# A fused linear-attention and expert layer: first and last batch reordered

## Chip, core and metric

One NeuronCore of a Trainium2 chip runs the whole program. The metric is the device time of one execution in microseconds (us), as the median of several executions. Engines are named as the profile names them: PE is TensorE, with PEld its weight loads; DVE is VectorE; ACT is ScalarE; POOL is GpSimd; SP is SyncE, which only issues DMAs here. All five run their own instruction streams and meet only at semaphores.

## What is computed

The input is x, 8 sequences x 2048 tokens x 256 channels, fp32. For each token:

```python
xn  = (x - mean(x)) / sqrt(var(x) + 1e-5)                 # over the 256 channels
q, k, v = split(xn @ wqkv);  q, k = relu(q), relu(k)      # 16 heads of 16
kv  = cumsum(k[..., :, None] * v[..., None, :], tokens)   # causal linear attention
y   = einsum('bhnd,bhnde->bhne', q, kv) / (einsum('bhnd,bhnd->bhn', q, cumsum(k)) + 1e-5)
s   = sigmoid(xn @ Wr)                                    # router, 8 experts, top 2, normalised -> cw
routed = sum over 4 MLP experts e of cw[e] * ((silu(xn @ Wg[e]) * (xn @ Wu[e])) @ Wd[e])
       + (cw[4] + cw[6]) * xn + cw[7] * relu(xn)
out = x + y @ wo + routed + causal_depthwise_conv4(xn)
```

## The kernel before

**Tiling.** The 16384 tokens go in 32 batches of 512 tokens (`BT`), four to a sequence; a batch is `T = 4` tiles of 128 tokens. Channels are `C = 2` halves of 128. `batch(s, j, left)` runs batch j of sequence s on each engine, and is written out by hand in program order for each engine (line 212, `rounds`). In each, the argument `k` of a helper says how far ahead of the batch it works: `heads(s, j, 1)` projects the next batch's queries, keys and values while the current one's output is being made.

**Precision.** Every fp32 product is made of three passes on fp32r data: each operand is split into a high part (ACT copies it, `high_weights`, `high_x`, `high_y`, `high_hid`) and a low part (the difference, `low_weights` on DVE; `low_x`, `low_y`, `low_hid` on POOL). `product` (line 296) issues the passes.

**A batch on PE** (lines 452 to 466): for each of the four tiles or experts t, `gate_up(t)` (12 matmuls of 512 columns), then `numerators(t)` (`state_sum`, 64 small matmuls with the masked scores, `state_sum`, 16 with the state). After tile 0 come the second half of the scores, after tile 1 the transposes of the next batch's xn (`turn_xn`). Then `heads` of the next batch, and four times `output(t)`: two transposes of the convolution `cT`, six matmuls with `wo`, twelve with `wd`. `state_sum(n)` waits until DVE has spread the running state into `state_bd` (`blocks(n)`).

**A batch on DVE** (lines 797 to 825): per tile `blocks`, `gate_up` (the product of silu and up), `blocks`, `attend` (line 792, numerator times inverse), and then in tile 0 `mask` of the second half of the scores (line 753), in tiles 1 to 3 `tap` (line 775, the convolution). Then, for later batches, `statistics` (line 689), `router`, `key_sums`, `products`, and between the final adds (line 825, `xb`) `inverses`, `mask`, `blocks`.

**A batch on ACT** (lines 559 to 577) does silu, the high parts, copies out of PSUM and the first tap; `heads` ends with the `same` terms (524), the relu terms (528, written over xn) and the denominators (531). **POOL** (lines 638 to 656) normalises the next batch, weighs the experts with `cwb` (626), makes low parts, and in `base` (614, 617) adds the terms into `x_t`.

**Ahead of the first batch.** SP issues, in this order, the first x block, tables, `wqkv` and router weights, three small tensors, gate and up weights, `wd`, `wo`, and x blocks 1 to 3. DVE runs `statistics` of batch 0, then `statistics` of batch 1 (line 836, which waits for x block 1), then all eight low parts of weights (839), then router, key sums, products, inverses, mask, blocks of batch 0. ACT makes the high parts of qkv weights, evicts the transposed xn (`fill_xT`), makes its high part from that, makes the other high weights, and goes on with `heads`. POOL normalises batch 0 after its own `rstd` (597), and makes `xl` (607). PE transposes xn (310), waits for the four qkv low parts (471), and runs `heads`.

**Behind the last batch.** PE's `output(0)` begins when all three taps are done (line 438); `x_t` of the batch is stored with one DMA of 512 KB (line 284) after the fourth final add.

Of the kernel before, what the change touches and what calls it, by code (L numbers as in the profile page):

```python
# [12 lines left out]
P = 128  # L13


def layer_kernel(nc, x, wqkv, wo, w_router, router_bias, w_gate, w_up, w_down, conv_w, conv_b,
# [28 lines left out]
    with ExitStack() as ctx:  # L45
# [31 lines left out]
        xn = sb("xn", [P, T, D])  # L77
# [91 lines left out]
        s_xn = sem("s_xn")  # L169
        s_xtr = sem("s_xtr")  # L170
# [68 lines left out]
        OWN_HEADS = 10 + 1 + 2 + 1  # L239
        OWN_SETUP = 2 * 2 + OWN_HEADS  # L240
        OWN_BODY = 2 + OWN_HEADS

# [3 lines left out]
        def _(sp):  # L246
            sp.dma_start(x_t[:, 0], x_v[0]).then_inc(x_in[0], 16)
            sp.dma_start(tables_s[:, :], tables).then_inc(tables_in, 16)
            sp.dma_start(st_r, w_router.rearrange("(c p) n -> p c n", p=P)).then_inc(qkv_in, 16)
            for c in range(C):  # L250
                sp.dma_start(st_qkv[:, c, :], wqkv[c * P:(c + 1) * P, :]).then_inc(qkv_in, 16)
            sp.dma_start(conv_ws[:, :, :], conv_w).then_inc(small_in, 16)
            sp.dma_start(conv_bs[:, :], conv_b).then_inc(small_in, 16)
            sp.dma_start(bias_s[:, :], router_bias).then_inc(small_in, 16)
# [5 lines left out]
            sp.dma_start(st_o, wo.rearrange("(c p) n -> p c n", p=P)).then_inc(out_in, 16)  # L260
            for j in range(1, BPS):
                sp.dma_start(x_t[:, j], x_v[j]).then_inc(x_in[j], 16)
# [16 lines left out]
            def batch(s, j, left):  # L279
# [3 lines left out]
                sp.wait_ge(s_out, at(s, j, T, 2 * T))  # L283
                sp.dma_start(out_v[b], x_t[:, j]).then_inc(stored, 16)
                sp.wait_ge(stored, at(s, j, 16, 16))
# [7 lines left out]
        def _(pe):  # L293
            mm = nc.tensor.matmul

            def product(dst, pairs, first=True, final=True):

                passes = [q for lh, ll, rh, rl in pairs for q in ((lh, rl), (lh, rh), (ll, rh))]
                for n, (lhs, rhs) in enumerate(passes):
                    ins = mm(dst, lhs, rhs, start=first and n == 0, stop=final and n == len(passes) - 1,  # L300
                             skip_group_check=not first)
                return ins

            def turn_xn(s, j, k, c):
                pe.wait_ge(s_xn, at(s, j, 1, k + 1))
                if k:

                    pe.wait_ge(s_sm, at(s, j, U * ROWS, U * ROWS))
                for t in range(T):
                    ins = nc.tensor.transpose(XB[c][:, t * P:(t + 1) * P], xn[:, t, c * P:(c + 1) * P], ident_s[:, :])  # L310
                ins.then_inc(s_xtr, 1)

            def heads(s, j, k):
# [15 lines left out]

                for g in range(C):  # L330
# [44 lines left out]
            def batch(s, j, left):  # L375
# [52 lines left out]
                def output(t):  # L428
# [8 lines left out]
                    if t == 0:  # L437
                        pe.wait_ge(s_conv, at(s, j, HALO, HALO))
                    for c in range(C):
                        mm(dst[:, c * P:(c + 1) * P], cT[:, c, ts], ident_s[:, :], is_transpose=True,  # L440
                           start=c == 0, stop=False, skip_group_check=True)
                    pe.wait_ge(s_yl, at(s, j, T, t + 1))
                    product(dst[:, 0:D], [(yh[:, c, ts], yl[:, c, ts], wo_h[:, c, :], wo_l[:, c, :])
                                          for c in range(C)], first=False, final=False)
                    for e in range(E):
                        if t == 0:
                            pe.wait_ge(s_hl, at(s, j, T, e + 1))
                        ins = product(dst[:, 0:D], [(hh[:, e, ts], hl[:, e, ts], wd_h[:, e, :], wd_l[:, e, :])],
                                      first=False, final=e == E - 1)
                    ins.then_inc(s_op, 1)  # L450
# [28 lines left out]
        def _(act):  # L479
# [25 lines left out]
            def heads(s, j, k):  # L505
# [13 lines left out]
                for g in range(C):  # L519
                    act.wait_ge(s_ktr, at(s, j, C, k * C + g + 1))  # L520
                    copy(ktok[:, :, g, :], KTB[g][:, :].rearrange("p (t n) -> p t n", t=T)).then_inc(s_ktok, 1)
                act.wait_ge(s_cw, at(s, j, 1, k + 1))
# [379 lines left out]
```

## Time and profile before

| | us |
|---|---|
| median of 3 runs (lowest, highest) | 1341.93 (1341.53, 1344.34) |
| the profiled execution's own time | 1342.8 |
| its span in the profile | 1341.0 |
| PE busy | 1310.1 (98%) |
| DVE busy | 1116.7 (83%) |
| POOL busy | 826.3 (62%) |
| ACT busy | 739.3 (55%) |

The span is from the first to the last recorded instruction or transfer; the own time has 1.8 us more around it. The chain that ended last is 97% PE. In the 40 slices PE shows 9 tenths in all but the first two (3, 8) and the last (7). A row of the timeline gives start, length, engine, line, operation, output<-input, shape, count, and in brackets the idle time of the engine before it and what ended it; the length of a merged row is from its first start to its last end.

### The profile page before, as it was taken

To read this page: it belongs to the slowest core of one execution; us is meant where nothing else is said; L and a number is where in the kernel's file an instruction comes from. 1 tells how busy PE (TensorE), PEld (TensorE's weight loads), DVE (VectorE), ACT (ScalarE), POOL (GpSimd) and SP (SyncE) were. 2 spreads that over 40 slices of the span, in tenths; PEclk is the share of its full clock that TensorE was granted. 3 is DMA by queue.
4 is the path that set the end of the run, shared out by engine and by line. 5 is a ranking of instruction groups with operands and counts; after the bars stand their busy time and mean duration, and the time that the engine had idled before them with its cause. 6 is when DMAs were issued, how large, how long until landed. Compare 5 with 4: busy or idle time off the path is not lost.

```text
span 1341.0 us, 54748 instructions
## 1 busy us (share of the span) xinstructions
PE 1310.1 (98%) x24384; PEld 1136.4 (85%) x24384; DVE 1116.7 (83%) x2566; ACT 739.3 (55%) x1545; POOL 826.3 (62%) x679
## 2 busy tenths in 40 slices
PE   3899999999999999999999999999999999999997
PEld 3788888888888888888888888888888888888886
DVE  4888898888888888988888988889888889888885
ACT  4555565455664565654556655555645556555561
POOL 2755666755766656657556666557576566575554
PEclk9999999999999999999999999999999999999999
DMA  4011111111111111011111111111112110111110
GB/s 148 34 66 65 51 48 34 66 65 66 44 55 34 66 66 64 35 38 61 66 65 50 50 35 65 66 65 37 63 34 66 65 64 35 34 65 50 50 49 18
DMA packets 46779, 73.73 MB, mean 55 GB/s; under 512 B 6480, under 2 KB 42192, under 8 KB 42448
## 3 DMA queue, kind: packets, MB, share of 16 engines
q1 hardware_dynamic: 46544, 70.24, 15.1%
q8 instruction: 191, 3.13, 1.0%
q14 instruction: 44, 0.36, 0.1%
HBM read 53.18 MB, written 17.04 MB: 52 GB/s over the span
## 4 chain that ended last, share of the span: by engine, by line
PE 97%; DVE 1%; SPq 1%; ACT 1%; DMA 1%; issue 0%; DVEq 0%
PE ring L300 51%; PE scores L300 17%; PE ring L408 7%; PE ring L424 6%; PE scores L357 5%; PE state_sum L371 4%; PE ring L440 2%; PE scores L310 2%; PE scores L339 2%; DMA x_t<-in_L_attn_x_dram 1%; SPq L257 0%; DVE cT L775 0%; DVE sm L753 0%; ACT qp L517 0%; ACT xn L528 0%
## 5 line engine op out<-in xcount | busy, mean ns | idle before, releaser
L626 POOL TENSOR_TENSOR hid<-hid,cwb 128x512 f32<-128x512 f32 x128 | 171.5, 1340 | 228.8 <-DVE hid L783 228.1
L775 DVE SCALAR_TENSOR_TENSOR cT<-xT,conv_ws,cT 128x512 f32<-128x512 f32 x192 | 292.9, 1564 | 0.0
L614 POOL TENSOR_TENSOR x_t<-x_t,same 128x1024 f32<-128x1024 f32 x32 | 77.0, 2406 | 258.6 <-ACT same L524 258.6
L760 DVE TENSOR_TENSOR state_bd<-state_sum,tables_s 128x256 f32<-128x256 f32 x248 | 103.7, 418 | 136.1 <-PE state_sum L371 136.1
L540 ACT ACTIVATE sg<-ring 128x512 f32<-128x512 f32 x128 | 76.6, 599 | 250.8 <-PE ring L300 250.8
L300 PE MATMUL ring<-xl,wgu_h 128*128 128x512 f32 x512 | 212.1, 414 | 0.0
L630 POOL TENSOR_TENSOR hl<-hid,hh 128x512 fp32r<-128x512 f32 x128 | 208.1, 1626 | 0.0
L300 PE MATMUL ring<-xh,wgu_l 128*128 128x512 f32 x512 | 202.7, 396 | 0.0
L300 PE MATMUL ring<-xh,wgu_h 128*128 128x512 f32 x512 | 202.0, 394 | 0.0
L480 ACT ACTIVATE yh<-yT 128x256 fp32r<-128x256 f32 x128 | 53.5, 418 | 247.3 <-DVE yT L792 247.3
L753 DVE TENSOR_TENSOR sm<-scores,causal_s 128x512 f32<-128x512 f32 x256 | 158.5, 679 | 22.3 <-PE scores L357 22.3
L300 PE MATMUL ring<-wd_h,hl 128*128 128x256 f32 x512 | 143.8, 281 | 0.0
L300 PE MATMUL ring<-wd_h,hh 128*128 128x256 f32 x512 | 143.6, 280 | 0.0
L300 PE MATMUL ring<-wd_l,hh 128*128 128x256 f32 x512 | 143.4, 280 | 0.0
L635 POOL TENSOR_TENSOR yl<-yT,yh 128x256 fp32r<-128x256 f32 x128 | 130.2, 1017 | 0.0
L408 PE MATMUL ring<-sm,vp 64*32 64x64 f32 x8192 | 118.8, 225 | 0.0
L300 PEld LDWEIGHTS ring<-xl,wgu_h 128*128 128x128 f32 x512 | 96.7, 189 | 24.5 <-issue 5.5
L300 PEld LDWEIGHTS ring<-xh,wgu_l 128*128 128x128 f32 x512 | 96.5, 188 | 22.4
L300 PEld LDWEIGHTS ring<-xh,wgu_h 128*128 128x128 f32 x512 | 97.1, 190 | 17.4
L371 PEld LDWEIGHTS state_sum<-vp,ktok 64*32 64x32 f32 x3968 | 54.1, 107 | 56.7 <-issue 51.5
L408 PEld LDWEIGHTS ring<-sm,vp 64*32 64x32 f32 x8192 | 98.1, 105 | 2.9 <-issue 2.9
L300 PE MATMUL scores<-xh,wqk_l 128*128 128x512 f32 x256 | 100.2, 392 | 0.0
(110 smaller groups left out, 3530.3 us busy)
## 6 DMA issues: line engine op xcount, KB each, us to landing
cwb<-cw_rows SPq DMA_DIRECT2D x32, 1024.0 KB, 4.6
x_t<-in_L_attn_x_dram SPq DMA_DIRECT2D x32, 512.0 KB, 4.3
out_dram<-x_t SPq DMA_DIRECT2D x32, 512.0 KB, 2.9
cw_rows<-cwt SPq DMA_DIRECT2D x128, 2.0 KB, 1.4
sm<-in_L_attn_wqkv_dram SPq DMA_DIRECT2D x2, 384.0 KB, 5.3
sm<-in_L_ffn_Wg_dram SPq DMA_DIRECT2D x2, 256.0 KB, 4.4
sm<-in_L_ffn_Wu_dram SPq DMA_DIRECT2D x2, 256.0 KB, 5.7
cwb<-in_L_ffn_Wd_dram SPq DMA_DIRECT2D x1, 512.0 KB, 4.4
```

What stands on the lines that cost most here:

```text
L300: ins = mm(dst, lhs, rhs, start=first and n == 0, stop=final and n == len(passes) - 1, skip_group_check=not first)
L371: ins = mm(ST[rows, g, :], ktok[toks, t, g, rows], vp[toks, t, g * PPG + m, 0:3:2, :], start=first and g == 0, stop=True, skip_group_check ...
L408: mm(NB2[t % 2][h][BLK * m:BLK * m + BLK, gs], window, sm[toks, t // 2, t % 2, 2 * pair + par, :], start=par == 0 and g == 0, stop=False, ...
L424: ins = mm(NB2[t % 2][h][rows, g * HALF:(g + 1) * HALF], state_bd[:, n % 4, cols], qT[:, g, n0:n0 + HALF], start=False, stop=True, skip_gr ...
L540: act.activation(sg[:, :], GB[t % 2], ACT.Silu).then_inc(s_sg, 1)
L614: pool.tensor_tensor(xb, xb, same[:, :, :], ALU.add).then_inc(s_base1, 1)
L626: pool.tensor_tensor(hid[:, e, :], hid[:, e, :], cwb[:, e, :], ALU.mult).then_inc(s_hid, 1)
L630: pool.tensor_tensor(hl[:, e, :], hid[:, e, :], hh[:, e, :].bitcast(F32), ALU.subtract).then_inc(s_hl, 1)
L635: pool.tensor_tensor(yl[:, :, t * P:(t + 1) * P], yT[:, t % 2, :, :], yh[:, :, t * P:(t + 1) * P].bitcast(F32), ALU.subtract).then_inc(s_y ...
L753: dve.tensor_tensor(heads, SB[f][:, :].rearrange("p (t a n) -> p t a n", a=2, n=HALF), causal2_s[:, :].unsqueeze(1).unsqueeze(1).to_broadc ...
L760: dve.tensor_tensor(state_bd[:, n % 4, :].rearrange("p (g m n) -> p g m n", g=C, m=PPG), ST.unsqueeze(2).to_broadcast([P, C, PPG, BLK]), s ...
L775: ins = dve.scalar_tensor_tensor(out=cT[:, c, :], in0=xT[:, j % 2, c, n:n + BT], scalar=conv_ws[:, c, n:n + 1], in1=cT[:, c, :], op0=ALU.m ...
```

## The change

- SP loads x block 0 and waits for it before it issues gate, up, `wd`, `wo`, the small tensors and x blocks 1 to 3. ACT issues tables, `wqkv` and router weights itself, at its start.
- `xn` has two halves, used by batches in turn. DVE normalises batch 0 tile by tile; PE transposes each tile as it comes. DVE and ACT evict the transposed xn from PSUM in parallel, `xT` by DVE and `xh` by ACT straight from PSUM, in opposite order of the halves. DVE makes `xl`.
- PE starts `heads` of batch 0 with two low parts of weights done and waits for the other two ahead of the keys.
- ACT runs one sigmoid on zeros at the start.
- `statistics` of batch 1 moves behind all low parts of weights; POOL normalises batch 1 ahead of `base` of batch 0 (in all later batches `normalise` stands at the end of a batch, behind `base`, where it stood at the beginning of the next).
- In batch 0, `inverses` moves from ahead of the first mask to a place between `blocks` and `attend` of tile 0; ACT's denominators follow silu(0), its relu terms follow the first tap.
- In the last batch, tap 3 goes ahead of `attend(3)`; `output(0)` adds the hidden products first, then the convolution, then the attention; the four tiles are stored one by one.

```diff
-        xn = sb("xn", [P, T, D])
+        xn = sb("xn", [P, 2, T, D])
...
             sp.dma_start(x_t[:, 0], x_v[0]).then_inc(x_in[0], 16)
-            sp.dma_start(tables_s[:, :], tables).then_inc(tables_in, 16)
-            sp.dma_start(st_r, w_router.rearrange("(c p) n -> p c n", p=P)).then_inc(qkv_in, 16)
-            for c in range(C):
-                sp.dma_start(st_qkv[:, c, :], wqkv[c * P:(c + 1) * P, :]).then_inc(qkv_in, 16)
-            sp.dma_start(conv_ws[:, :, :], conv_w).then_inc(small_in, 16)
...
+            sp.wait_ge(x_in[0], 16)
             for src, dst in ((w_gate, st_g), (w_up, st_u)):
...
+            sp.dma_start(conv_ws[:, :, :], conv_w).then_inc(small_in, 16)
...
+                    for t in range(T):
+                        sp.wait_ge(s_out, at(s, j, T, T + t + 1))
+                        sp.dma_start(out_v[b][:, t, :], x_t[:, j, t, :]).then_inc(stored, 16)
+                    sp.wait_ge(stored, at(s, j, 16, 16 * T))
...
+            def turn_first():
+
+                for t in range(T):
+                    pe.wait_ge(s_xn_tile, t + 1) if t < T - 1 else pe.wait_ge(s_xn, 1)
+                    for c in range(C):
+                        ins = nc.tensor.transpose(XB[c][:, t * P:(t + 1) * P], xn[:, 0, t, c * P:(c + 1) * P],
+                                                  ident_s[:, :])
+                        if t == T - 1:
+                            ins.then_inc(s_xtr, 1)
...
+                if not k:
+                    pe.wait_ge(w_split, EARLY)
                 for g in range(C):
                     project(KB[g][:, :], D + g * P).then_inc(s_kp, 1)
...
+                    late = last and t == 0
...
+                    if late:
+                        add_hidden()
+                        turn_conv()
+                        add_attention().then_inc(s_op, 1)
+                    else:
+                        turn_conv()
+                        add_attention()
+                        add_hidden().then_inc(s_op, 1)
...
-            for c in range(C):
-                turn_xn(0, 0, 0, c)
-            pe.wait_ge(w_split, EARLY)
+            turn_first()
+            pe.wait_ge(w_split, 2)
             heads(0, 0, 0)
...
                 silu(0)
+                if s == j == 0:
+                    denominators(0, 0, 0)
                 first_tap()
+                if s == j == 0:
+                    relu_terms(0, 0, 0)
...
+            act.dma_start(tables_s[:, :], tables).then_inc(tables_in, 16)
+            for c in range(C):
+                act.dma_start(st_qkv[:, c, :], wqkv[c * P:(c + 1) * P, :]).then_inc(qkv_in, 16)
+            act.dma_start(st_r, w_router.rearrange("(c p) n -> p c n", p=P)).then_inc(qkv_in, 16)
+            act.wait_ge(set_up, 3)
+
+            act.activation(sg[:, 0:1], zeros[:, 0:1], ACT.Sigmoid)
...
             high_weights(SPLITS[:EARLY])
-            act.wait_ge(set_up, 3)
-            fill_xT(0, 0, 0)
-            high_x(0, 0, 0)
+            for c in range(C):
+                act.wait_ge(s_xtr, c + 1)
+                if c:
+
+                    act.wait_ge(s_xT, 1)
+                copy(xh[:, 0, c, :], XB[c][:, :]).then_inc(s_xh, 1)
             high_weights(SPLITS[EARLY:])
...
-                if not last:
-                    normalise(s, j, 1)
                 weigh(0)
...
                 if not last:
                     base(s, j, 1)
+                if left > 1:
+                    normalise(s, j, 2)
...
-            normalise(0, 0, 0)
-            for c in range(C):
-                low_x(0, 0, 0, c)
-            pool.wait_ge(tables_in, 16)
+            inverse_deviation(0, 0, 0)
+            normalise(0, 0, 1)
             base(0, 0, 0)
...
+                    if s == j == t == 0:
+                        inverses(0, 0, 0)
+                    early = last and t == T - 1
+                    if early:
+                        tap(t)
                     attend(t)
                     if t == 0:
                         mask(s, j, 0, 1)
-                    else:
+                    elif not early:
                         tap(t)
...
             statistics(0, 0, 0)
-            statistics(0, 0, 1)
...
-            low_weights(0, N_SPLITS)
-            dve.wait_ge(small_in, 16 * 3)
+            dve.wait_ge(s_rstd, 1)
+            for t in range(T):
+                dve.tensor_scalar(xn[:, 0, t, :], x_t[:, 0, t, :], negm[:, t:t + 1], rstd[:, t:t + 1], ALU.add,
+                                  ALU.mult).then_inc(s_xn_tile if t < T - 1 else s_xn, 1)
+            low_weights(0, 2)
+            for c in (1, 0):
+                dve.wait_ge(s_xtr, C)
+                if c == 0:
+
+                    dve.wait_ge(s_xh, 1)
+                ins = dve.tensor_scalar(xT[:, 0, c, HALO:HALO + BT], XB[c][:, :], 1.0, None, ALU.mult)
+                ins.then_inc(s_xT, 1)
+            for c in range(C):
+                dve.wait_ge(s_xT, C)
+                dve.wait_ge(s_xh, c + 1)
+                dve.tensor_tensor(xl[:, 0, c, :], xT[:, 0, c, HALO:HALO + BT], xh[:, 0, c, :].bitcast(F32),
+                                  ALU.subtract).then_inc(s_xl, 1)
+            low_weights(2, N_SPLITS)
...
+            dve.wait_ge(small_in, 16 * 3)
+            statistics(0, 0, 1)
             router(0, 0, 0)
             key_sums(0, 0, 0)
             products(0, 0, 0)
-            inverses(0, 0, 0)
             mask(0, 0, 0, 0)
             blocks(0, 0, 0, 1)
```

## Rows read from the trace of the kernel before

**Rows 1.** Stretch of one batch: us, busy time of each engine, clock, DMA share, GB/s.

```profile
81.70:122.50 40.80, 40.80 (x770) 35.40 (x769) 35.16 (x80) 22.83 (x48) 25.55 (x22) 1.00 0.16 54
```

**Rows 2.** Waits of PE over the span: total us, times, longest us.

```profile
PE scores L310 <- POOL xn L600: 10.0, 1, 10.0
PE scores L300 <- DVE wqk_l L833: 9.3, 1, 9.3
PE ring L440 <- DVE cT L775: 3.1, 1, 3.1
PE scores L357 <- ACT ktok L480: 2.3, 1, 2.3
...
```

**Rows 3.** Timeline of the first 27 us, all engines.

```profile
4.30 1.41 DVE L689 BATCH_NORM_STATS2 stats<-x_t 128x6 f32<-128x256 f32 x4 [4.30 <-DMA x_t<-in_L_attn_x_dram]
...
7.68 2.16 POOL L600 TENSOR_SCALAR xn<-x_t,negm,rstd 128x256 f32<-128x256 f32 x4
...
8.97 0.63 ACT L480 ACTIVATE wvr_h<-sm 128x512 fp32r<-128x512 f32 x1 [6.97 <-DMA sm<-in_L_attn_wqkv_dram]
...
9.98 1.94 PE L310 MATMUL scores<-tables_s,xn 128*128 128x128 f32 x8 [9.98 <-POOL xn L600]
...
12.45 1.14 ACT L480 ACTIVATE xh<-xT 128x512 fp32r<-128x512 f32 x2
...
15.68 1.06 ACT L480 ACTIVATE wd_h<-cwb 128x1024 fp32r<-128x1024 f32 x1 [0.20 <-DMA sm<-in_L_attn_wo_dram]
...
17.19 1.41 DVE L689 BATCH_NORM_STATS2 stats<-x_t 128x6 f32<-128x256 f32 x4 [10.79 <-DMA x_t<-in_L_attn_x_dram]
...
23.39 1.22 DVE L833 TENSOR_TENSOR wd_l<-cwb,wd_h 128x1024 fp32r<-128x1024 f32 x1
...
26.79 0.19 DVE L700 TENSOR_TENSOR scoreb<-score,bias_s 128x32 f32<-128x32 f32 x1 [1.20 <-ACT score L509]
```

**Rows 4.** Timeline of DVE, 33 to 50 us.

```profile
34.92 1.28 DVE L738 TENSOR_REDUCE den<-qks_tok 128x32 f32<-128x512 f32 x2
38.24 0.55 DVE L744 RECIPROCAL rden<-dene 128x64 f32<-128x64 f32 x1 [2.04 <-ACT dene L531]
...
40.05 2.44 DVE L753 TENSOR_TENSOR sm<-scores,causal_s 128x512 f32<-128x512 f32 x4
...
45.73 2.48 DVE L753 TENSOR_TENSOR sm<-scores,causal_s 128x512 f32<-128x512 f32 x4 [0.68 <-PE scores L357]
49.00 0.42 DVE L760 TENSOR_TENSOR state_bd<-state_sum,tables_s 128x256 f32<-128x256 f32 x1 [0.79 <-PE state_sum L371]
```

**Rows 5.** Timeline of PE, 42 to 50 us.

```profile
42.98 0.25 PE L371 MATMUL state_sum<-vp,ktok 64*32 64x32 f32 x7 [2.17 <-DVE state_bd L760]
...
45.62 0.51 PE L300 MATMUL ring<-xl,wgu_h 128*128 128x512 f32 x1
...
49.48 0.33 PE L371 MATMUL state_sum<-vp,ktok 64*32 64x32 f32 x16
```

**Rows 6.** Timeline of DVE and POOL behind the last attention tile.

```profile
1323.36 2.61 DVE L775 SCALAR_TENSOR_TENSOR cT<-xT,conv_ws,cT 128x512 f32<-128x512 f32 x2
...
1323.70 1.71 POOL L630 TENSOR_TENSOR hl<-hid,hh 128x512 fp32r<-128x512 f32 x1
...
1326.51 1.28 POOL L630 TENSOR_TENSOR hl<-hid,hh 128x512 fp32r<-128x512 f32 x1
```

**Rows 7.** The chain that ended last, in order of time: PE in `output(0)`.

```profile
1326.77 3.24 PE ring L300 x18
```

**Rows 8.** DMA issues of the page: count, KB each, median us to landing.

```profile
out_dram<-x_t SPq DMA_DIRECT2D x32, 512.0 KB, 2.9
cw_rows<-cwt SPq DMA_DIRECT2D x128, 2.0 KB, 1.4
```

**Rows 9.** Timeline of DVE in a middle batch, tile 3.

```profile
711.33 0.42 DVE L760 TENSOR_TENSOR state_bd<-state_sum,tables_s 128x256 f32<-128x256 f32 x1 [0.33 <-PE state_sum L371]
...
712.92 3.40 DVE L775 SCALAR_TENSOR_TENSOR cT<-xT,conv_ws,cT 128x512 f32<-128x512 f32 x2
```

More of the change, by code:

```diff
@@ L300, in product @@
                     ins = mm(dst, lhs, rhs, start=first and n == 0, stop=final and n == len(passes) - 1,
-                             skip_group_check=not first)
+                             skip_group_check=not (first and final))
                 return ins
@@ L436, in output @@
                         pe.wait_ge(s_sig, at(s, j, T, T + 2 + t))
-                    if t == 0:
-                        pe.wait_ge(s_conv, at(s, j, HALO, HALO))
-                    for c in range(C):
[L440 to L444, printed above, removed]
@@ L445, in output, with turn_conv @@
-                    for e in range(E):
-                        if t == 0:
[L447 to L450, printed above, removed]
+                    late = last and t == 0
+                    def turn_conv():
+                        if t == 0:
+                            pe.wait_ge(s_conv, at(s, j, HALO, HALO))
+                        for c in range(C):
+                            mm(dst[:, c * P:(c + 1) * P], cT[:, c, ts], ident_s[:, :], is_transpose=True,
+                               start=c == 0 and not late, stop=False, skip_group_check=True)
@@ new lines, in add_hidden, with add_attention @@
+                    def add_hidden():
+                        for e in range(E):
+                            if t == 0:
+                                pe.wait_ge(s_hl, at(s, j, T, e + 1))
+                            ins = product(dst[:, 0:D], [(hh[:, e, ts], hl[:, e, ts], wd_h[:, e, :], wd_l[:, e, :])],
+                                          first=late and e == 0, final=e == E - 1 and not late)
+                        return ins
+                    def add_attention():
+                        pe.wait_ge(s_yl, at(s, j, T, t + 1))
+                        return product(dst[:, 0:D], [(yh[:, c, ts], yl[:, c, ts], wo_h[:, c, :], wo_l[:, c, :])
+                                                     for c in range(C)], first=False, final=late)
@@ L667, in _, with own @@
         def _(dve):
-            count = {"setup": 0, "body": 0, "in_body": False}
-            def own(ins, s, j, apart=False):
+            steps = itertools.count(1)
+            def own(ins, apart=False):
                 ins.then_inc(s_own, 1)
-                if not count["in_body"]:
-                    count["setup"] += 1
-                    dve.wait_ge(s_own, count["setup"])
-                else:
-                    count["body"] += 1
-                    dve.wait_ge(s_own, s * (BPS * OWN_BODY) + (j * OWN_BODY + count["body"] + OWN_SETUP))
+                dve.wait_ge(s_own, next(steps))
                 if apart:
@@ L725, in key_sums @@
                                                  before, ALU.add, ALU.add)
-                own(ins, s, j)
+                own(ins)
             def products(s, j, k):
@@ L743, in inverses @@
                 dve.wait_ge(s_dene, at(s, j, 1, k + 1))
-                own(dve.reciprocal(rden[:, :, :], dene[:, :, :]), s, j)
+                own(dve.reciprocal(rden[:, :, :], dene[:, :, :]))
                 for g in range(C):
@@ L825, in batch @@
                     dve.tensor_tensor(xb, OB[t][:, 0:D], xb, ALU.add).then_inc(s_out, 1)
-                if left > 1:
-                    assert count["body"] == OWN_BODY, count
             def low_weights(first, stop):
```

78 lines of the change are left out of this document (44 added, 34 removed).

## The prediction

> **What bounds the kernel now.** I read the busy times first, then the busy time of single batches, then PE's waits, then the timelines of the first 50 us and of the last 20. A middle batch takes 40.80 us and PE is busy for all of it, at a granted clock of 1.00 [rows 1]. PE's list of waits has five entries in the whole span, each met once: 10.0, 9.3, 3.1 and 2.3 us [rows 2] and 2.2 [rows 5], 26.9 in all. Four of them lie ahead of 43 us, one at the end. So nothing off PE matters in the 31 batches between, and the change can win only in the first 43 us and in the last 18. The reader should see in the timeline which chain ends each of these waits:
>
> - PE could transpose at 9.98, when POOL had normalised all four tiles [rows 3].
> - It then stood until 21.26 (9.98 + 1.94 + 9.34) for the low part of the qkv weights. DVE had nothing to do for 10.79 us, because the statistics of batch 1 stood ahead of the weights in its queue and waited for x block 1 until 17.19 [rows 3].
> - It stood 2.2 us until 42.98 for `state_bd`, behind DVE's inverses (from 38.24) and mask (from 40.05) [rows 4, 5].
> - At the end it stood 3.1 us for tap 3, which ended at 1325.97 (1323.36 + 2.61) [rows 6].
>
> **The start of `heads`.** Before, 21.26. After, it follows this chain.
>
> 1. x block 0 lands. Before 4.30 [rows 3]. Now ACT's queue has tables and `wqkv` in flight beside it from the first moment. Ends: 4.30 (tables were in flight before as well), and 8.97, when ACT found `wqkv` there [rows 3], if x came last of them all. I take 4.9, near the first, since SP still issues it first and waits before it adds anything.
> 2. Statistics, `rstd` and their semaphores take 3.38 (4.30 to 7.68) [rows 3]: 8.3.
> 3. Four normalisations on DVE. No row has this operation there. Upper end 0.54 each, POOL's own (2.16 / 4) [rows 3]; lower end 0.11, a quarter of a 128x256 `state_bd` at 0.42 [rows 4]. I take 0.25, total 1.0: 9.3.
> 4. The transposes follow tile by tile, 0.24 each (1.94 / 8) [rows 3]; two are left after the last tile: 9.8. `wvr_l` on DVE is through at 10.2 if `wqkv` has landed by 7.5 or so, and at the latest at 11 if it still lands at 8.97.
> 5. Two evictions on either engine side by side. ACT's of 128x512 is 0.57 (1.14 / 2) [rows 3]. DVE's has the mask as its nearest row, 0.61 a piece (2.44 / 4, also out of PSUM) [rows 4]. With two semaphores 1.3: 11.5. Then two `xl` of 128x512 with two SBUF inputs, each half of the 1.22 of `wd_l` [rows 3] and a little more, 1.4: 12.9.
>
> So `heads` starts at 13.0, 8.3 us earlier, with ends 11.5 and 16. From there to the end of the first `gate_up` is 19.55 (21.26 to 42.98 - 2.17) [rows 5], with its own 2.3 us wait for `ktok` [rows 2] in it, since that is ACT's own chain of eight copies and does not change. PE is at the end of `gate_up` at 32.5.
>
> **DVE's chain decides instead.** PE now waits for `state_bd`, and DVE has more queued ahead of it than PE has.
>
> 1. `wd_h` starts when `wd` and `wo` have landed, 15.68 [rows 3]. The same bytes stand ahead of them as before, so I keep it; ends 14 and 18.
> 2. `wd_h` 1.06, then `wd_l` to the end of the two small products, 23.39 to 25.59 (26.79 less the 1.20 of idle time), 2.2 [rows 3]: 18.95. The other low parts are done before that. x block 1, landed at 17.19 before [rows 3], is now behind three small loads; up to 19 it costs nothing.
> 3. `statistics` of batch 1, 2.1 (to the first low part of weights, 17.19 to 19.3): 21.1. This is the piece that the change moves from a place where it blocked PE to one where it blocks the router. Scores are there earlier (13.0 + 4.8 and ACT's four copies).
> 4. Router to the end of the denominators 9.41 (26.79 to 36.20) [rows 3, 4]: 30.5.
> 5. Mask and `blocks` to PE's restart 2.93 (40.05 to 42.98) [rows 4, 5]: 33.4.
> 6. POOL normalises batch 1 at this moment, beside router and key sums; before, both ran with POOL idle. What POOL and DVE cost one another is seen at the end: the same `hl` takes 1.71 beside a tap and 1.28 alone [rows 6]. Which side pays in the router no row shows. Lower end 0, upper end the whole 2.16 of POOL's xn [rows 3]; I take 0.7.
>
> PE restarts at 34.1 against 42.98: **8.9 us**. The Trainium skill ("SBUF — State Buffer", section "Who interferes with whom") states that a DVE instruction with two SBUF inputs and a GpSimd instruction that reads SBUF cannot run together, the second waiting for the first to finish. By that rule each small product of the router could wait for up to one normalised tile; with three of them caught for half a tile each the estimate is 0.8 instead of my 0.7. The trace agrees in kind, 1.71 against 1.28.
>
> **What the moved inverses give back.** They stand now between `blocks` and `attend` of tile 0. Their length is 1.81 (38.24 to 40.05) [rows 4]. `attend(0)`, the instruction ahead of the second mask, was done at 45.05 (45.73 - 0.68) [rows 4], 2.07 after PE's restart, and becomes about 3.9; PE needs it for the second half of `gate_up(1)`, six matmuls of 0.23 after 45.62 [rows 5], that is 4.0 after the restart, so it just hides. The second mask began 2.75 after the restart and now begins at 3.9: 1.15 late. The `state_bd` behind it had 0.79 of idle time [rows 4], so it is 0.35 late, and the `state_sum` that needs it began the moment it could, at 49.48, 0.06 after `state_bd` ended [rows 5]. **Minus 0.3**. ACT's relu terms fill an idle 3.6 us between the first tap and high_y(0); POOL's second `base` and weigh(0) come 2.6 us later against the restart, but `hh` and `hl` of expert 0 are wanted 35 us later. Nothing.
>
> **The middle.** On POOL the order `base`, `normalise`, `weigh(0)` is what it was; the loop boundary moved, not the instruction. DVE, ACT, PE and SP issue the same in the same order. Nothing, 31 times.
>
> **The end.** Tap 3 goes ahead of `attend(3)`, which then ends at 1325.3, and PE starts `output(0)` at 1325.4 in place of 1326.1, because its bank is free only after `attend(3)`. But `hl` of expert 3 is late next: `yh(3)`, `yl(3)`, then 1.28 of `hl` [rows 6], ready at about 1327.8 as before, while nine hidden matmuls at the 0.18 of that stretch (3.24 / 18) [rows 7] are through at 1327.0. PE stands up to 0.8, and after it eleven of the twenty are left, 2.0, ending at 1329.8 against 1330.0 (1326.77 + 3.24): the early start is nearly all given back. **0.2**, ends -0.5 and 0.7. The last store shrinks from 512 KB to 128 KB. 512 KB land after 2.9 us, 2 KB after 1.4 [rows 8]; on that line 128 KB take 1.8. **1.1**, ends 0 and 1.5. The three other stores are issued while PE works.
>
> **Sum.** 8.9 - 0.3 + 0.2 + 1.1 = 9.9 us. The profiled execution took 1342.8 with a span of 1341.0, so it would be 1332.9 with 1331.1. It lies 0.9 above the median, 1341.93, from which the forecast is **1332.0 us**.
>
> **Rivals.**
>
> - *The first loads collide.* SP's and ACT's loads share the same transfer time, x block 0 lands late, and SP, which now waits for it, issues gate, up, `wd` and `wo` late as well, so that both chains shift. For it: all loads up to 17 us kept the DMA engines busy. Against it: SP's next loads were issued at 4.6 us before, which is no earlier than x block 0 can land. If x block 0 lands at 7 rather than 4.9, `wd` and x block 1 come some 2.5 later and PE restarts at 36.6: 1334.5. The Trainium skill ("DMA: Bandwidth & Descriptors", section "Issuing engines are not separate DMA queues") says that DMAs from different engines interleave on the same 16 DMA engines and that a second issuer saves only issue time. By that rule x block 0 is no longer ahead of everything. The trace agrees so far that x block 0 shared with tables before.
> - *DVE's chain is shorter.* `wd` and `wo` land sooner since x blocks 1 to 3 are issued behind the small loads, and POOL costs nothing beside the router. Then DVE is at 32.3, PE's own chain (32.5) decides, and the whole is 1330.3.
> - *Slower than before: the middle batches lose a little each.* Place: DVE's `state_bd` in tile 3, which waits only 0.33 us for PE [rows 9] and follows a tap. The pair of taps costs 2.61 with little beside it and 3.40 with much [rows 6, 9]. If the new halves of xn let POOL run in step with tap 2, DVE is late by 0.79 - 0.33 = 0.46 in each of 31 batches, 14.3 us: 1346.3. It decides from 0.32 us a batch (9.9 / 31). Against it: POOL's order has no place in which to run earlier.
> - *It does not do what it says.* The start gained is lost before batch 1, since another input of batch 0 is late, above all the `cwb` spread through DRAM, which ended about 7 us after the router. It would be at 31.2, and POOL wants it at 35. For 1341 it would have to be 9 us later.
>
> **How the numbers follow.** Forecast 0.58, its own range 1330.8 to 1333.5; first loads collide 0.18; shorter DVE chain 0.18; slower 0.03; no effect 0.03. The range 1329.4 to 1335.2 takes in the first three with their bounds. A measurement of this kernel tells about 0.2% (2.7 us) from no change. Faster by more than that needs less than 1339.2: 0.95. Same 0.02, slower 0.03.
>
> **What would show it.** PE's first `heads` matmul near 13; DVE's idle time of 10.8 gone and its second statistics ending at 21; PE's restart at the first `state_bd` near 34 with about 1.5 us of wait; a wait of some 0.3 at the third `state_sum`; batches of 40.80; PE waiting for `hl` in `output(0)` for 0.5 or more; a last store landing after 1.8. I am wrong if PE waits in batch 1 or later, if `heads` starts after 16, or if PE's restart is bound by its own chain and not by `state_bd`.

## The result, and the profile after

The changed kernel takes 1335.12 us as the median of 6 runs (1334.10 to 1335.33), the kernel before 1344.47 in 6 (1341.53 to 1347.43). The ratio is 0.9934, with a 95% interval of 0.9922 to 0.9947: 7 to 10.5 us less. Forecast were 9.9 less, and 1332.0 with its own range 1330.8 to 1333.5 and a wide one of 1329.4 to 1335.2. The direction and nearly the size are right; the time lies above the own range and just inside the wide one. Of 3.1 us between the two times, 2.5 are that the kernel before also ran slower than in its first three runs. The profiled execution took 1334.1, the least of the six, with a span of 1332.3, 8.7 under that of before. Its parts ("that tile" is the last attention tile of the last batch):

| part | forecast | profile | from |
|---|---|---|---|
| restart of PE in batch 0 | 8.9 | 9.2 | 42.98 to 33.77 |
| inverses moved | -0.3 | -0.35 | third `state_sum` 6.85 after the restart, was 6.50 |
| 31 middle batches | 0 | -0.65 | last attention tile ends 8.21 earlier, third `state_sum` 8.86 |
| order of the last batch | 0.2 | -0.8 | last final add 15.0 after that tile, was 14.2 |
| store by tiles | 1.1 | 1.3 | from that add to the end 2.54, was 3.84 |

The rows behind the last three lines, of the kernel before and then of the changed one:

```profile
1322.28 0.69 PE L424 MATMUL ring<-qT,state_bd 128*64 128x64 f32 x16
...
1337.16 0.42 DVE L825 TENSOR_TENSOR x_t<-ring,x_t 128x256 f32<-128x256 f32 x1 [1.91 <-PE ring L300]
```

```profile
1314.07 0.69 PE L439 MATMUL ring<-qT,state_bd 128*64 128x64 f32 x16
...
1329.76 0.42 DVE L883 TENSOR_TENSOR x_t<-ring,x_t 128x256 f32<-128x256 f32 x1 [1.92 <-PE ring L303]
```

The waits of PE in the changed kernel answer to [rows 2]. None is for `state_bd` any more, and two are new and stand in `output(0)` of the last batch.

```profile
PE scores L321 <- DVE xn L896: 8.9, 1, 8.9
PE scores L303 <- DVE xl L909: 2.8, 1, 2.8
PE scores L372 <- ACT ktok L511: 2.3, 1, 2.3
PE ring L303 <- DVE yT L845: 2.1, 1, 2.1
PE ring L303 <- POOL hl L691: 1.3, 1, 1.3
```

A stretch of one batch, as in [rows 1]: still 40.80 us of PE in 40.80.

```profile
70.00:110.80 40.80, 40.80 (x769) 35.38 (x769) 35.03 (x81) 22.85 (x48) 25.58 (x22) 1.00 0.16 54
```

The timeline of the start, all engines, answers to [rows 3]. x block 0 lands 0.76 later than before, DVE normalises in 1.38, `heads` begins at 13.67, and DVE is in the router at 21.16.

```profile
5.06 1.41 DVE L743 BATCH_NORM_STATS2 stats<-x_t 128x6 f32<-128x256 f32 x4 [5.06 <-DMA x_t<-in_L_attn_x_dram]
...
8.38 1.38 DVE L896 TENSOR_SCALAR xn<-x_t,negm,rstd 128x256 f32<-128x256 f32 x4 [1.20 <-POOL rstd L655]
...
10.91 1.29 DVE L904 TENSOR_SCALAR xT<-scores 128x512 f32<-128x512 f32 x2 [0.47 <-PE scores L321]
...
12.23 1.29 DVE L909 TENSOR_TENSOR xl<-xT,xh 128x512 fp32r<-128x512 f32 x2
...
13.67 0.56 PE L303 MATMUL scores<-wvr_l,xh 128*128 128x264 f32 x1 [2.80 <-DVE xl L909]
...
14.30 1.06 ACT L511 ACTIVATE wd_h<-cwb 128x1024 fp32r<-128x1024 f32 x1
...
19.15 1.41 DVE L743 BATCH_NORM_STATS2 stats<-x_t 128x6 f32<-128x256 f32 x4
...
21.16 0.18 DVE L754 TENSOR_TENSOR scoreb<-score,bias_s 128x32 f32<-128x32 f32 x1
...
22.73 0.35 DVE L764 TENSOR_TENSOR hot<-hot 128x32 f32<-128x32 f32 x1
```

The restart, DVE and PE together [rows 4, 5]. DVE has `state_bd` ready at 33.63; PE ends its last gate matmul at 33.79. In this execution the two chains end together.

```profile
29.63 1.28 DVE L792 TENSOR_REDUCE den<-qks_tok 128x32 f32<-128x512 f32 x2
...
33.22 0.41 DVE L814 TENSOR_TENSOR state_bd<-state_sum,tables_s 128x256 f32<-128x256 f32 x1
...
33.39 0.40 PE L303 MATMUL ring<-xh,wgu_l 128*128 128x512 f32 x1
...
33.77 0.25 PE L386 MATMUL state_sum<-vp,ktok 64*32 64x32 f32 x7
...
40.15 0.41 DVE L814 TENSOR_TENSOR state_bd<-state_sum,tables_s 128x256 f32<-128x256 f32 x1
...
40.62 0.33 PE L386 MATMUL state_sum<-vp,ktok 64*32 64x32 f32 x16
```

The end [rows 6, 7], PE, POOL and DVE. PE begins 2.1 us after the attention tile (ended 1314.76), has nine hidden matmuls done at 1318.3, and stands until 1319.62 for `hl` of expert 3.

```profile
1316.89 0.39 PE L303 MATMUL ring<-wd_l,hh 128*128 128x256 f32 x1 [2.13 <-DVE yT L845]
...
1318.04 0.28 PE L303 MATMUL ring<-wd_h,hl 128*128 128x256 f32 x1
1318.29 1.27 POOL L691 TENSOR_TENSOR hl<-hid,hh 128x512 fp32r<-128x512 f32 x1
1319.62 0.58 PE L303 MATMUL ring<-wd_l,hh 128*128 128x256 f32 x1 [1.30 <-POOL hl L691]
```

The same end in stretches (length, busy time of PE, PEld, DVE, ACT, POOL, granted clock, DMA): the nine matmuls run at the 2.4 GHz level, all that comes behind the wait until 1322.4 at the 1.2 GHz level.

```profile
1317.00:1318.00 1.00, 1.00 (x8) 0.97 (x9) 0.00 (x0) 0.81 (x2) 1.00 (x2) 1.00 0.00 0
...
1320.00:1321.00 1.00, 1.00 (x6) 1.00 (x6) 0.00 (x0) 0.00 (x0) 0.00 (x0) 0.50 0.00 0
```

The four last stores among the DMA issues, against [rows 8]: 1.7 us to landing in the median.

```profile
out_dram<-x_t SPq DMA_DIRECT2D x4, 128.0 KB, 1.7
```

### The profile page after: what moved, and what is told of

It is laid out like the page before. It is cut to its first block, busy times and chain, and to the rows that moved or that the text cites. A ratio compares the mean times of both kernels' runs of the same rounds, so it can differ in the third digit from the quotient of the medians.

```text
span 1332.3 us, 54753 instructions
## 1 busy us (share of the span) xinstructions
PE 1312.0 (98%) x24384; PEld 1136.9 (85%) x24384; DVE 1120.6 (84%) x2574; ACT 737.4 (55%) x1543; POOL 822.7 (62%) x673
## 4 chain that ended last, share of the span: by engine, by line
PE 97%; DVE 1%; POOL 0%; ACT 0%; DMA 0%; issue 0%; POOLq 0%; DVEq 0%
PE ring L303 51%; PE scores L303 17%; PE ring L423 7%; PE ring L439 6%; PE scores L372 5%; PE state_sum L386 4%; PE ring L459 2%; PE scores L312 2%; PE scores L354 2%; DMA x_t<-in_L_attn_x_dram 0%; DVE cT L828 0%; ACT qp L548 0%; DVE sm L807 0%; PE scores L321 0%; POOL hid L687 0%
## 5 line engine op out<-in xcount | busy, mean ns | idle before, releaser
L303 PEld LDWEIGHTS ring<-xh,wgu_h 128*128 128x128 f32 x512 | 97.2, 190 | 17.5
```

## The experiments

Each edit is against the changed kernel, unless it says otherwise. Medians stand beside a run of the kernel before in the same job, between 1342.5 and 1344.1. Where only a span is given (gate_first, pool_low, norm_late, no_sp_wait), there was one execution; what is read from it are times of single rows, not its whole time.

**The end as before (start_alone).** The conditions of the two new orders are switched off, and the store is one DMA.

```diff
-                    late = last and t == 0
+                    late = False
-                    early = last and t == T - 1
+                    early = False
-                if left:
+                if True:
                     sp.wait_ge(s_out, at(s, j, T, 2 * T))
```

> The changed kernel with its last batch as before (tap 3 after attend(3), output(0) with the convolution first and the hidden products last, one store of 512 KB). Theory: from the last attention tile to the end of output(0) the new order costs PE 0.5 us and output(1) another 0.3, since PE stands 1.3 us for hl of expert 3 after nine matmuls at full clock and does the rest at half clock; the four stores are worth 1.3. Then this kernel has output(0) over 6.9 us after the last attention tile as in the kernel before, output(1) in 2.4, the last store 3.4 from the final add to the end, and a span of 1332.3 - 0.8 + 1.3 = 1332.8. Rival: the order is worth the 0.2 forecast and the loss lies ahead of the last batch: then 1332.3 + 0.2 + 1.3 = 1333.8. Both expect the small shift in the middle batches, 0.02 us a batch, again if it belongs to the new start.

Measured: 1334.39 us (5 runs), ratio 0.9932 (0.9918 to 0.9946), span 1333.3, own time not told from that of the changed kernel. From the attention tile (ended 1315.16) the last final add comes after 14.3 us and the end after 18.1, in the changed kernel after 15.0 and 17.5: the store wins 1.3 and the new order loses 0.7 of it, and what is left, 0.6, is too little for the times to tell. So the theory holds for the order. It fails for `output(1)`, which was to take 2.4 and took 2.7 here too: the slow matmuls at its start do not belong to the new order. The span lies between theory and rival because the middle differed too: PE's 31st transposes stood 7.89 us ahead of those of before, having been 8.78 ahead in the first batch. The timeline of PE and DVE:

```profile
1318.29 0.41 PE L459 MATMUL ring<-tables_s,cT 128*128 128x128 f32 x2 [3.14 <-DVE cT L828]
...
1329.50 0.42 DVE L883 TENSOR_TENSOR x_t<-ring,x_t 128x256 f32<-128x256 f32 x1 [1.91 <-PE ring L303]
```

**Expert 3 last (hid3_last).**

```diff
                     if late:
-                        add_hidden()
+                        add_hidden(range(E - 1))
                         turn_conv()
-                        add_attention().then_inc(s_op, 1)
+                        add_attention()
+                        add_hidden([E - 1]).then_inc(s_op, 1)
```

> The changed kernel, but output(0) of the last batch adds the hidden products of experts 0 to 2, then convolution and attention, and expert 3 last. Theory (the loss at the end is the order of work around one late operand, and the clock that falls in the wait): 17 instructions run at full clock from 1316.9 to about 1319.0, PE waits 0.6 for hl of expert 3, three matmuls follow, output(0) ends near 1320.2 instead of 1322.1 and the clock stays up for output(1), 2.4 us; span about 1330.2. Rival (the clock falls in any case, because PE was idle 2.1 us before output(0)): the wait shrinks, the slow matmuls stay, output(0) ends near 1321.2, span 1331.2 or more.

Measured: 1331.63 us (5 runs), ratio 0.9914 (0.9900 to 0.9928), span 1330.7; 3.5 us under the changed kernel by medians of different jobs, 2.7 by the two ratios, 1.6 by the two spans. The wait for `hl` is gone from PE's list, and so is the wait's price: the last final add comes 13.5 us after the tile (1314.65 to 1328.13). On the clock the theory was wrong and the rival right, though the end of `output(0)` (1320.8) and the span lie between the two: it fell at 1317.3, in the midst of the matmuls. In PE's timeline the 256-column matmul goes from 0.28 to 0.41 and back.

```profile
1317.02 0.28 PE L303 MATMUL ring<-wd_h,hh 128*128 128x256 f32 x1
...
1317.48 0.41 PE L303 MATMUL ring<-wd_h,hh 128*128 128x256 f32 x1
...
1320.66 0.28 PE L303 MATMUL ring<-wd_h,hl 128*128 128x256 f32 x1
```

**Three outputs woven (end_woven).** Against the changed kernel. Two things differ in the last batch: PE works on three outputs in turn, and DVE does tap 3 behind `attend(3)` again, as before the change.

```diff
-                    if late:
-                        add_hidden()
+                    if part == 0:
+                        add_hidden(range(2))
+                        add_attention()
+                    elif part == 1:
                         turn_conv()
-                        add_attention().then_inc(s_op, 1)
+                        add_hidden(range(2, E)).then_inc(s_op, 1)
...
+                if last:
+                    for t in range(T - 1):
+                        output(t, 0)
+                    for t in range(T - 1):
+                        output(t, 1)
+                    output(T - 1)
...
-                    early = last and t == T - 1
+                    early = False
```

> The changed kernel with another last batch: attend(3) goes ahead of tap 3 again, and PE adds to the outputs of tiles 0, 1 and 2 first experts 0 and 1 and the attention, then to the three of them convolution and experts 2 and 3, then does tile 3. Theory (the loss at the end is one late operand met early: the last tap at +3.0 us and hl of expert 3 at +4.8 us after the last attention tile, and the clock that falls while PE waits): PE has 4.3 us of work that needs neither, waits at most 0.5 for attend(3) and under 1 for yl, the clock stays up, and the last final add begins 10.4 to 11.4 us after the last attention tile, against 15.0 in the changed kernel and 14.2 before; span 1327.7 to 1328.8. Rival (the clock falls in this batch in any case): 1.7 us more of slow matmuls, 12.1 to 13, span near 1330.

Measured: 1328.94 us (4 runs), ratio 0.9897 (0.9880 to 0.9914), span 1327.6. It beats both kernels. PE waits 0.53 once, the clock stays up, and the last final add begins 10.3 us after the attention tile (1314.83 to 1325.09), 4.7 sooner than in the changed kernel and 3.9 sooner than before. How much of this is the weaving and how much the earlier `attend(3)` was not run apart. A row of PE's timeline and one of DVE's:

```profile
1315.35 0.39 PE L303 MATMUL ring<-wd_l,hh 128*128 128x256 f32 x1 [0.53 <-DVE yT L854]
...
1325.09 0.42 DVE L892 TENSOR_TENSOR x_t<-ring,x_t 128x256 f32<-128x256 f32 x1 [1.91 <-PE ring L303]
```

And the stretch in which PE stood before:

```profile
1318.00:1320.00 2.00, 2.00 (x19) 2.00 (x19) 0.00 (x0) 0.00 (x0) 1.70 (x2) 1.00 0.00 0
```

**Statistics of batch 1 ahead again (stats_ahead).**

```diff
+            statistics(0, 0, 1)
             low_weights(0, 2)
...
-            statistics(0, 0, 1)
             router(0, 0, 0)
```

> The changed kernel with the statistics of batch 1 ahead of the low parts of weights and of the evictions again, where they wait for x block 1. Theory: this one wait holds the whole gain. x block 1 lands near 17, statistics end at 19.4, low part of wv and router 0.8, evictions and xl 2.7: heads starts at 23.2, PE restarts near 43.3, span 1341.8. Rival (the gain is shared with the other edits of the start, parallel evictions, loads in order, normalisation on DVE): heads starts near 17, span about 1336.

Measured: 1341.61 us (10 runs), ratio 0.9984 (0.9974 to 0.9994), span 1340.4. The theory holds, with 1.4 too high a span: x block 1 landed at 16.16 and not near 17, `heads` started at 21.67 and not 23.2. PE's transposes of the next batch stand at 48.60, in the changed kernel at 41.49 and before at 50.35, so undoing this one move gives back 7.1 of 8.9 us. The move alone, in the kernel before, was not run. DVE, then PE:

```profile
16.16 1.41 DVE L743 BATCH_NORM_STATS2 stats<-x_t 128x6 f32<-128x256 f32 x4 [6.23 <-DMA x_t<-in_L_attn_x_dram]
...
21.67 0.56 PE L303 MATMUL scores<-wvr_l,xh 128*128 128x264 f32 x1 [10.62 <-DVE xl L910]
```

**Inverses ahead of the mask again (inverses_back).** `inverses(0, 0, 0)` stands behind `products`, the denominators end ACT's `heads`.

```diff
-                    if s == j == t == 0:
-                        inverses(0, 0, 0)
...
             products(0, 0, 0)
+            inverses(0, 0, 0)
             mask(0, 0, 0, 0)
```

> The changed kernel with the inverses of batch 0 (and the denominators on ACT) ahead of the first mask again. Theory: DVE reaches the mask 1.9 to 2.1 us later, PE's restart moves from 33.8 to 35.8, and the wait of 0.35 at the third state_sum and of 0.1 in gate_up(1) go: net 1.6 us slower, span 1333.9. Rival (the two chains of PE and DVE ended together at 33.8, and each of the two waits behind it gives back what the restart lost): under 0.5 us slower.

Measured: 1337.75 us (4 runs), ratio 0.9955 (0.9938 to 0.9972), span 1335.8. The restart moved to 36.04, 0.2 past the 35.8 expected, but the transposes of the next batch came at 44.59, 3.1 us late and not 1.6, more than either theory or rival said. Behind the 2.0 us wait the clock went down, and the scores took 1.91 instead of 1.21. PE's timeline:

```profile
36.04 0.25 PE L386 MATMUL state_sum<-vp,ktok 64*32 64x32 f32 x7 [2.01 <-DVE state_bd L813]
...
38.01 1.91 PE L372 MATMUL scores<-qp,kT 32*64 32x128 f32 x64
```

And a stretch behind the wait, with its granted clock of 0.50:

```profile
37.00:38.00 1.00, 1.00 (x42) 0.83 (x26) 0.88 (x2) 0.00 (x0) 1.00 (x1) 0.50 0.06 16
```

**Two chains at the restart (gate_first, pool_low, gate_pool).** All three stand on the kernel with expert 3 last. The first shortens PE's chain, the second was to shorten DVE's, the third does both.

```diff
...
             heads(0, 0, 0)
+            pe.wait_ge(w_split, N_SPLITS)
+            pe.wait_ge(s_sig, T)
+            gate_up_of(0, 0, 0)
             scores(0, 0, 0, 0)
...
```

```diff
-            low_weights(2, N_SPLITS)
+            low_weights(2, N_SPLITS - 2)
...
             inverse_deviation(0, 0, 0)
+            for n in range(N_SPLITS - 2, N_SPLITS):
+                _, _, hi, lo, src = SPLITS[n]
+                pool.wait_ge(w_hi, n + 1)
+                pool.tensor_tensor(lo, src, hi.bitcast(F32), ALU.subtract).then_inc(w_pool, 1)
```

> The kernel with expert 3's hidden products last, and PE does gate_up(0) of batch 0 ahead of the first scores instead of behind them, so that it works through its 2.3 us wait for ktok. Theory: two chains end together at PE's restart, PE's own (end of gate_up at 33.6) and DVE's (state_bd ready at 33.65); shortening PE's alone gives nothing: restart at 33.6 to 33.9, now with a wait of about 4 us for state_bd. Rival (PE's own chain decides, DVE's has room): restart near 32.

> The kernel with expert 3's hidden products last, and POOL instead of DVE makes the low parts of wd and wo in the start. Theory: DVE's chain gets 1.5 to 1.9 us shorter (router waits for the last score near 19.7), but PE's own chain ends at 33.6 as before and the restart stays at 33.6 to 33.9. Rival (DVE's chain decides alone): restart near 32.

> Both edits together. Theory (two chains that end together): only now the restart moves, to about 32.5: router at 19.7, denominators at 29.3, mask until 32.1 with the scores ready at 29.6. PE then waits 2.5 us for state_bd, and the clock may fall in that wait, which would give back up to 1.7; span 1330.7 - 1.2 = 1329.5. Rival (another input of the first mask or of PE ends at the same time as well): restart above 33.3.

Measured: span 1331.0, 1334.7 and 1333.1 (gate_pool 1334.90 us in 6 runs, ratio 0.9935, 0.9921 to 0.9948). The first is as expected: restart at 33.97, now with a wait of 5.1, and behind it a slow stretch that puts the next transposes at 42.41. So PE finishing sooner gains nothing; DVE's chain holds it. The kernel that this edit stands on shows the same without it: in hid3_last, whose start is the changed kernel's, PE's gate matmuls were done 1.07 us ahead of `state_bd`, and the restart was at 33.88.

```profile
33.88 0.25 PE L386 MATMUL state_sum<-vp,ktok 64*32 64x32 f32 x7 [1.07 <-DVE state_bd L815]
```

The other two are misses, for a reason that neither theory had. Timeline of DVE and POOL in pool_low:

```profile
14.64 4.54 DVE L897 TENSOR_TENSOR wgu_l<-sm,wgu_h 128x1024 fp32r<-128x1024 f32 x2
...
15.21 2.89 POOL L728 TENSOR_TENSOR wd_l<-cwb,wd_h 128x1024 fp32r<-128x1024 f32 x1 [6.88 <-ACT wd_h L515]
...
28.52 3.48 DVE L794 TENSOR_TENSOR qks<-qT,ksum 128x512 f32<-128x512 f32 x2
...
28.61 2.85 POOL L679 TENSOR_TENSOR x_t<-x_t,same 128x1024 f32<-128x1024 f32 x1 [2.37 <-ACT same L561]
...
37.52 0.25 PE L388 MATMUL state_sum<-vp,ktok 64*32 64x32 f32 x7 [4.55 <-DVE state_bd L822]
```

The two `wgu_l` take 2.35 with POOL idle and 4.54 beside POOL's `wd_l`; the two `qks` 1.29 and, when DVE's lateness brings them beside POOL's `base`, 3.48. Both times DVE loses 2.2 us to one POOL instruction of 2.9. The restart was at 37.52. In gate_pool POOL's `base` (29.70, 2.36 long) came behind the two `qks`; they kept their own length, and the restart was at 35.31, 2.2 sooner. The two rows with POOL idle, from the changed kernel and from gate_pool:

```profile
14.65 2.35 DVE L889 TENSOR_TENSOR wgu_l<-sm,wgu_h 128x1024 fp32r<-128x1024 f32 x2
```

```profile
28.49 1.29 DVE L801 TENSOR_TENSOR qks<-qT,ksum 128x512 f32<-128x512 f32 x2
```

Whether both chains shortened together move the restart was therefore not tested.

**POOL's normalisation away from the router (norm_late).**

```diff
             inverse_deviation(0, 0, 0)
-            normalise(0, 0, 1)
             base(0, 0, 0)
...
+                if s == j == k == 0:
+                    normalise(0, 0, 1)
                 pool.wait_ge(s_base1, at(s, j, 1, k + 1))
```

> The changed kernel with POOL's normalisation of batch 1 moved from beside the router of batch 0 to behind the first addition of its base, beside the first mask. Theory (two-input products of DVE wait for POOL's instruction that reads SBUF): from the first instruction of the router to the end of the denominators 9.42 instead of 9.75 us; the restart of PE stays at its own chain's end, 33.6 to 33.8. Rival (the 0.33 is chance from execution to execution): 9.75 again.

Measured: span 1331.6. From the router to the end of the denominators 9.40 (21.28 to 29.40 + 1.28), against 9.75 (21.16 to 30.91): the theory's 9.42, not the rival's 9.75. The restart came at 33.61. Two small products of two inputs in SBUF have their own length again, `hot` 0.19 for 0.35 and `c` 0.12 for 0.28. It is not chance: `hot` takes 0.35 also in inverses_back, no_sp_wait, pool_low and gate_pool, where POOL normalises beside it, and 0.19 in stats_ahead, where POOL is done by then.

```profile
21.28 0.19 DVE L755 TENSOR_TENSOR scoreb<-score,bias_s 128x32 f32<-128x32 f32 x1
22.85 0.19 DVE L765 TENSOR_TENSOR hot<-hot 128x32 f32<-128x32 f32 x1
...
29.40 1.28 DVE L793 TENSOR_REDUCE den<-qks_tok 128x32 f32<-128x512 f32 x2
```

**Without SP's wait (no_sp_wait).**

```diff
             sp.dma_start(x_t[:, 0], x_v[0]).then_inc(x_in[0], 16)
-            sp.wait_ge(x_in[0], 16)
```

> The changed kernel without SP's wait for x block 0 between that load and the next ones. Theory: ACT's loads are what x block 0 shares the transfers with, and it landed at 5.06 instead of 4.30; SP's next loads add to that, x block 0 lands at 5.5 to 6.5, heads and PE's restart come later by the same 0.5 to 1.4. Rival (x block 0's transfers are all started before the next are issued, the wait only delays the weights): x block 0 at 5.1, weights 0.5 sooner, restart the same.

Measured: span 1332.4; x block 0 at 5.03, restart at 33.75. The rival holds: `wd` landed 0.6 and `wo` 1.2 sooner, and the wait neither costs nor brings anything at the restart. Here too PE stood for `state_bd`, 1.06 us.

```profile
5.03 1.41 DVE L742 BATCH_NORM_STATS2 stats<-x_t 128x6 f32<-128x256 f32 x4 [5.03 <-DMA x_t<-in_L_attn_x_dram]
...
33.75 0.25 PE L385 MATMUL state_sum<-vp,ktok 64*32 64x32 f32 x7 [1.06 <-DVE state_bd L813]
```

## Where the prediction held and where it failed

**The start held.** The step was "DVE had nothing to do for 10.79 us, because the statistics of batch 1 stood ahead of the weights": stats_ahead shows that undoing this order gives back 7.1 of 8.9 us. Such shares overlap: undoing the move of the inverses lost another 3.1 of the same 8.9. The chain to `heads` was 0.67 longer than forecast (13.0, measured 13.67). DVE came to the evictions 0.24 late (x block 0 landed 0.16 later than taken, a normalisation took 0.35 and not 0.25) and then waited 0.47 for the transposes. That wait is a slip of step 4: at 0.24 each, the two transposes of a tile take 0.48, longer than a normalisation, so PE falls behind and has more than two left after the last tile; its eight ran without a gap from 8.93 to 10.87, where the forecast had 9.8.

**"DVE's chain decides instead" held in part, and its number with luck.** DVE came to the router at 21.16, as forecast. But `wd` and `wo` had landed by 14.3, not 15.68; what held DVE was its own queue. POOL beside the router cost 0.35 where I took 0.7. So DVE's chain ended at 33.6 instead of 34.1. PE's chain was forecast for 32.5 and ended at 33.79: it started 0.67 late, and at the lower clock `heads` took 10.8 instead of 10.3 and `gate_up` 4.5 instead of 4.0, while the scores were 0.5 quicker. The 1.5 us of wait for `state_bd` that I named as a sign did not come. The sign of being wrong, a restart bound by PE's own chain, stands at the edge: the restart follows `state_bd` by 0.14, as it does where PE waits (0.15 before the change), but PE could have gone only some 0.06 sooner, since its last gate matmul began 0.38 ahead of the restart where 0.32 is usual. Other executions fall on either side of it. With the same start, hid3_last has a wait of 1.07 for `state_bd` and no_sp_wait, which leaves out SP's wait, one of 1.06, with restarts at 33.88 and 33.75; in end_woven and norm_late PE's chain was the last, at 33.89 and 33.61. DVE had `state_bd` ready at 33.6 to 33.7 each time, at 33.4 in norm_late, and where PE's ends depends on where the clock rises. Of the rivals, the late x block 0 (7 us) did not come, and the shorter DVE chain had its premise right, `wd` and `wo` sooner, and its result wrong.

**The moved inverses held**: -0.35 against -0.3, 0.1 of it in `gate_up(1)` and the rest at the third `state_sum`. What undoing the move costs was mis-sized: beside the later restart, the clock behind its wait cost 1.2 us (8.55 from the restart to the next transposes, 7.37 before the change).

**The failed step is the end.** I wrote that "the early start is nearly all given back" and put down a gain of 0.2; it is a loss of 0.8. I had the late operand (`hl` of expert 3), its time (4.8 after the tile, as before) and the wait. The wait was 1.3 and not 0.8, because PE began 0.3 sooner than taken and the nine matmuls needed 1.4 and not 1.6; by itself that moves nothing, since the wait ended when forecast. The mis-sized term is the work behind it: eleven instructions at 0.18, 2.0 us. That 0.18 of [rows 7] is a mean over both clock levels; behind the wait all eleven ran at the lower one and took 2.5, and the start of `output(1)` another 0.3. In all PE stood 3.4 us in two waits, where it had stood 3.1 in one.

Nor is the 15.0 us from the tile to the last final add a fixed price. Four other executions have this same order of the last batch, and they took 15.1 (norm_late), 15.1 (inverses_back), 15.8 (no_sp_wait) and 16.3 (stats_ahead); the first final add came 7.5 to 7.7 after the tile in all five, and the rest is how long the clock stayed low in `output(1)`. The old order took 14.2 and 14.3, expert 3 last 13.4 to 13.6 in four executions, the woven order 10.3 in one. The last final adds of the two longest (tiles ended 1314.09 and 1321.57):

```profile
1329.89 0.42 DVE L882 TENSOR_TENSOR x_t<-ring,x_t 128x256 f32<-128x256 f32 x1 [1.91 <-PE ring L302]
```

```profile
1337.84 0.42 DVE L883 TENSOR_TENSOR x_t<-ring,x_t 128x256 f32<-128x256 f32 x1 [1.91 <-PE ring L303]
```

The profiled execution of the changed kernel is the shortest of these five and also the shortest of its own six; that the others lost their 0.2 to 1.2 us in `output(1)` is likely and not shown. Why the clock rises sooner in one execution than in another stays open.

An order that puts ready work first gains only if that work lasts until the late operand comes. The nine matmuls put first did not (1.4 us of work for 2.7 from PE's start); the first parts of three tiles did (4.3), and end_woven is 4.7 us ahead of the changed kernel and 3.9 ahead of the order before.

**The middle.** The 0.65 us there does not come with the change's code. Against the kernel before, the lead of PE's transposes falls from batch 1 to 31 by 0.60 in the changed kernel, 0.89 in start_alone, 0.87 in inverses_back, 0.54 in end_woven, 0.40 in hid3_last and 0.28 in stats_ahead; it changes by less than 0.1, and grows, in gate_first, pool_low, gate_pool, no_sp_wait and norm_late, all with the same middle. What makes single executions 0.01 to 0.03 us a batch slower stays open. Without it the changed kernel's span would have been 1331.7, 0.6 above the forecast 1331.1. So the nearness of the sum is in part luck: the restart and the store came 0.3 and 0.2 better than forecast and hid part of 1.0 at the end.

## What to carry to other kernels

In a kernel whose one engine is full, list its waits, and for each the queue in which the operand it waits for stood behind something that waited itself; undoing one such move, that of the statistics, gave back 7.1 of 8.9 us here. Before putting ready work ahead of a late operand, add up whether the ready work lasts until it comes; if not, take it from the next tiles as well. Do not give an idle engine work whose reads shut the busy one out.

## What the runs showed of the hardware

- A VectorE instruction with both inputs in SBUF stood while a GpSimd instruction on SBUF ran: 2.35 became 4.54 and 1.29 became 3.48, each beside one GpSimd instruction of 2.9. It is not always VectorE that stands: in stats_ahead GpSimd's four normalisations, 2.2 us in the other kernels, came while VectorE made low parts of two inputs and took 7.7 (one of them 3.1), and the two `wgu_l` beside them kept their 2.35. VectorE work with one input in PSUM did not change: the mask took 2.48 in norm_late with GpSimd busy nearly all through it, and 2.48 in gate_pool with GpSimd idle. The Trainium skill ("SBUF — State Buffer", section "Who interferes with whom") says that a DVE instruction with two SBUF inputs contends with a GpSimd instruction that reads SBUF, that one with at most one SBUF input does not, and that the contention is an exclusive lock. The traces agree, and more plainly than the 1.71 against 1.28 of [rows 6] had let me expect.
- The granted clock fell in or behind waits of 2.0 to 5.3 us, and sometimes only in the midst of the work behind them: at 1317.3 in hid3_last, 0.5 us after PE had begun again. In end_woven, with a wait of 0.5, it stayed up. Length alone does not tell: before the change the wait of 2.2 at the restart cost no clock; in inverses_back one of 2.0 did.
- Stores of 128 KB landed after 1.7 us, those of 512 KB after 2.9, both in the median.
